# Copying x with its upper half already shifted by a token, one transpose per batch, and feed-forward weights loaded inside the layer

## The chip, the cores and the metric

The kernel runs on one core of one Trainium2 chip. A core has a matrix engine (PE in the profile; PEld is its weight load), a vector engine (DVE), a scalar engine (ACT), a GpSimd engine (POOL) and a sync engine (SP) that here only issues DMAs. Each runs its own instruction stream in order and waits on semaphores. The metric is device time in microseconds (us), lower is better.

## The reference, cut to what matters

The program is a small transformer: x is 16 batches of 128 tokens by 128 features. A first attention, a mixture of experts and a second cross-attention come first (about the first quarter of the time). Then come six layers, which the change is about:

```python
def shift_tokens(t):
    a, s = jnp.split(t, 2, -1)
    s = jnp.pad(s, ((0, 0), (1, 0), (0, 0)))[:, :-1]
    return jnp.concatenate([a, s], -1)
...
for i in range(DEPTH):                       # DEPTH = 6
    x = attn_layer(shift_tokens(x), Wqkv[i], q_scale[i], k_scale[i], Wo[i]) + x
    x = ffn_layer(shift_tokens(x), ln_g[i], ln_b[i], W1[i], b1[i], W2[i], b2[i]) + x
```

`attn_layer` projects to q, k and v (16 heads of 64), normalises q and k, applies rotary tables, attends in windows of 32 tokens to the own window and the one before, and projects back. `ffn_layer` is layer norm, a gated hidden layer of 341 features, and a projection back. `shift_tokens` leaves features 0 to 63 of a token and takes features 64 to 127 from the token before; token 0 gets zeros.

## The kernel before, in words

`Y` holds x in on-chip memory, tokens on the partitions. In each layer the attention goes through 64 units: a unit is one of the 16 batches and four of the 16 heads. On each engine a `Pipeline` lays out the stages of a unit, each stage some slots behind the first, so that one slot of PE holds a stage of each of several units. A layer is: 8 opening slots written out (`nxt.start(...)`, the first four of them woven into the feed-forward part of the layer before), a loop of 7 turns of 8 slots (`att.steady()`), and the closing slots woven into the feed-forward part of the same layer. That feed-forward part works on 4 groups of 4 batches. The layers 0 to 4 are the body of an outer loop (`Fori(0, LAYERS - 1)`) which begins with `att.steady()`; the last layer is written out behind it.

The PE order within a slot is: scores (mask L850, products L858), transposes of q and k (L831, 4), probabilities times values (`l_pv`, L878, 32 small products), projection of q and k (L814), of v (L823), output projection (L898), transposes of the result (L888, 2), transposes of the probabilities (L841, 2), and in every fourth slot `l_turn_x` (L802 and L803). `l_turn_x` reads `xin`, a copy of one batch of `Y`, and puts its transpose into the bank: the lower 64 features by a product with the identity, the upper 64 by a product with a shifted identity, which is the token shift. ACT and DVE split the turned x into two parts for the projections.

SP serves the layers by a written-out order (`serve_layer`). Per batch it issues twice four DMAs that move values to other partitions (`move_values`, L360: `stash<-l_v`), as soon as ACT has copied the v of two units (L1179), and one DMA `xin<-Y` (`take_x`, L365) for the batch after next. PE's `l_pv` of every second unit waits for the four moves. During the first three batches of a layer SP also loads the projection weights of the next layer (L330). After the last batch it waits for the output projections, loads `l_wo`, waits for the first feed-forward group, copies x of two batches of the next layer, then waits until all four feed-forward groups are done and issues the 12 DMAs of the next layer's feed-forward weights (`load_feed_forward`, L336 to L347). Only behind these come the first `move_values` of the next layer. The engines wait for these weights (`ld_fw`) at the start of the feed-forward part of the layer.

Of the kernel before, what the change touches and what calls it, by code (L numbers as in the profile page):

```python
# [20 lines left out]
B, S, D = 16, 128, 128  # L21
HALF = D // 2
# [68 lines left out]
def build(nc, t, out):  # L91
    with ExitStack() as ctx:
        def sb(name, shape, dt=F32):
            return ctx.enter_context(nc.sbuf_tensor(name, shape, dt))

        def sem(name):
            return ctx.enter_context(nc.semaphore(name))

        def upto(before, n):

            return before + (max(n, 0) if isinstance(n, int) else n) + CREDIT


        bank = ctx.enter_context(nc.psum_tensor("bank", [128, 8, 512], F32))
        X = sb("X", [128, B, D])
        Y = sb("Y", [128, B, D])
# [6 lines left out]
        ident = const[:, K_IDENT:K_IDENT + 128]  # L115
        shift_t = const[:, K_SHIFT:K_SHIFT + 128]
# [93 lines left out]
        xin = sb("xin", [128, 2, D])  # L210

        l_ss = sb("l_ss", [128, 2, 8, 2])
# [29 lines left out]
        preset = sem("preset")  # L242
        moved = [[sem(f"moved{k}{q}") for q in range(2)] for k in range(2)]
        ld_xin = [sem(f"ld_xin{k}") for k in range(2)]
# [8 lines left out]
        def stage_sems(prefix, names):  # L253

            made = {n: sem(prefix + n) for n in names.split()}
            stage_all.extend(made.values())
            return made
# [9 lines left out]
        l = stage_sems("l_", core.replace("sub_done ", "") + "w_high_done w_split "  # L267
                 "x_turned x_high_done x_split qk_proj v_proj rot_done sq_done ss_done floored logged guessed newton rn_done "
                 "add_done qk_done qk_turned qkT_done v_done o_turned oT_done out_done res_done")
        f = stage_sems("f_", "xs stats stat pool_st rstd n_done turned nT_done hidden gelu_done h_done out_mm yb_done "  # L270
                 "y_done")
# [3 lines left out]
        def apart(eng):  # L275


            eng.sem_inc(passed[eng.engine], 1)

        def one(t3, b):  # L280

            return t3[:, bass.ds(b, 1), :].rearrange("p a n -> p (a n)")
# [3 lines left out]
        def _(sp):  # L286
# [35 lines left out]
            def layer(name, ly):  # L322
                x = t["L1_ffn_" + name]
                v = x[bass.ds(ly, 1)]
                return v.rearrange("a b c -> (a b) c") if len(x.shape) == 3 else v.rearrange("a b -> (a b)")

            def load_projections(ly, *pieces):
                for piece in pieces:
                    at = slice(512 * piece, 512 * piece + 512)
                    sp.dma_start(l_raw[:, at], layer("Wqkv", ly)[:, at]).then_inc(ld_raw, 16)  # L330

            def load_output(ly):
                sp.dma_start(l_wo[:], layer("Wo", ly).rearrange("(c p) n -> p c n", p=128)).then_inc(ld_lw, 16)

            def load_feed_forward(ly):
                sp.dma_start(f_w1[:], layer("W1", ly)).then_inc(ld_fw, 16)  # L336
                full = FF // 128 * 128
                sp.dma_start(f_w2[:, 0:full // 128, :],
                             layer("W2", ly)[0:full].rearrange("(c p) n -> p c n", p=128)).then_inc(ld_fw, 16)
                sp.dma_start(f_w2[0:FF - full, full // 128, :], layer("W2", ly)[full:FF]).then_inc(ld_fw, 16)  # L340
                sp.dma_start(f_g[:, 0:1], layer("ln_g", ly).rearrange("(p a) -> p a", a=1)).then_inc(ld_fw, 16)
                sp.dma_start(f_g[:, 1:2], layer("ln_b", ly).rearrange("(p a) -> p a", a=1)).then_inc(ld_fw, 16)
                for s in range(2):
                    for k, (c0, n) in enumerate(CHUNKS):
                        sp.dma_start(f_b1[0:n, s, k:k + 1], layer("b1", ly)[s * FF + c0:s * FF + c0 + n]
                                     .rearrange("(p a) -> p a", a=1)).then_inc(ld_fw, 16)
                sp.dma_start(f_b2[:], layer("b2", ly).partition_broadcast(128)).then_inc(ld_fw, 16)  # L347

            def move_values(ly, b, k, q):

                ub, two = ly * UNITS, slice(2 * q, 2 * q + 2)
                sp.wait_ge(l["v_done"], upto(ub, 4 * b + 2 * q + 2))
                apart(sp)
                if not isinstance(b, int) or b >= 2:
                    sp.wait_ge(l["pv_done"], upto(ub, 4 * b + 2 * q - 6))
                    apart(sp)
                for dst, half, at in ((l_v2, 0, 32), (l_v2, 1, 32), (l_v3, 0, 64), (l_v3, 1, 0)):
                    sp.dma_start(dst[64 * half:64 * half + 64, k, two], l_v[at:at + 64, k, half, two])\  # L360
                      .then_inc(moved[k][q], 16)

            def take_x(ly, b, k):

                sp.dma_start(xin[:, k], one(Y, b)).then_inc(ld_xin[k], 16)  # L365

            def next_x(ly, b, k):
                sp.wait_ge(l["x_turned"], upto(ly * B, b + 1))
                apart(sp)
                take_x(ly, b + 2, k)  # L370

            def serve_layer(ly, last):

                for b in range(4):
                    for q in range(2):
                        move_values(ly, b, b % 2, q)
                        if q == 0:
                            next_x(ly, b, b % 2)
                        if not last and 2 * b + q < W_CHUNKS:
                            if b + q == 0:  # L380
                                sp.wait_ge(l["w_split"], upto(0, (ly + 1) * W_CHUNKS))
                                apart(sp)
                            load_projections(ly + 1, 2 * b + q)
                with sp.Fori(2, B // 2 - 1) as i:
                    for k in range(2):
                        move_values(ly, 2 * i + k, k, 0)
                        next_x(ly, 2 * i + k, k)
                        move_values(ly, 2 * i + k, k, 1)
                for b in range(B - 2, B):
                    for q in range(2):  # L390
                        move_values(ly, b, b % 2, q)
                if not last:
                    sp.wait_ge(l["out_done"], upto(0, (ly + 1) * B))
                    apart(sp)
                    load_output(ly + 1)
                    sp.wait_ge(f["y_done"], upto(0, ly * 4 + 1))
                    apart(sp)
                    for b in range(2):
                        take_x(ly + 1, b, b)
                    sp.wait_ge(f["y_done"], upto(0, (ly + 1) * 4))  # L400
                    apart(sp)
                    load_feed_forward(ly + 1)

            load_projections(0, *range(W_CHUNKS))
            load_output(0)
            load_feed_forward(0)
            sp.wait_ge(c["y_done"], upto(0, 2))
            for b in range(2):
                take_x(0, b, b)
            sp.wait_ge(c["y_done"], upto(0, B))  # L410
            with sp.Fori(0, LAYERS - 1) as ly:
                serve_layer(ly, False)
# [10 lines left out]
        def _(pool):  # L423
# [2 lines left out]
            pool.memset(c_v[:, :, :, :, C_DIM:], 1.0)  # L426
            pool.memset(l_v[:, :, :, :, :, L_DIM:], 1.0)
            pool.memset(m_p[:, :, EXPERTS:], -1.0)
            pool.memset(l_ss[:, :, :, 1:], 1e-24).then_inc(preset, 1)
            pool.wait_ge(preset, 1)  # L430

            def rstd(dst, var, chain, n, done):
# [158 lines left out]
        def _(pe):  # L591
# [180 lines left out]
            def attention(ly):  # L772
                ub, bb = ly * UNITS, ly * B

                def issued(mine, other, r):

                    at = [fn for _, fn in stages]
                    (s0, _), (s1, _) = stages[at.index(mine)], stages[at.index(other)]
                    return r + s0 - s1 + (at.index(other) < at.index(mine))
# [4 lines left out]
                def values_read(mine, b, r):  # L784

                    v, x = (issued(mine, fn, r) for fn in (l_project_v, l_turn_x))
                    pe.wait_ge(l["v_done"], upto(ub, no_more(4 * b + v, UNITS)))
                    pe.wait_ge(l["x_split"], upto(bb, no_more(b + (x + 3) // 4, B)))
# [5 lines left out]
                    pe.wait_ge(l["oT_done"], upto(ub, no_more(4 * b + turned, UNITS)))  # L794

                def l_turn_x(u, b, j):

                    if j % 4 == 0:
                        x = xin[:, j // 4]
                        pe.wait_ge(ld_xin[j // 4], (ly * B + b - j // 4) * 8 + 16)  # L800
                        values_read(l_turn_x, b, 0)
                        pe.matmul(bank[0:HALF, 1, 256:384], x[:, 0:HALF], ident, start=True, stop=True)  # L802
                        pe.matmul(bank[HALF:, 1, 256:384], x[:, HALF:], shift_t, start=True, stop=True)\  # L803
                          .then_inc(l["x_turned"], 1)

                high, low = (w[:].rearrange("p (t n) -> p t n", t=3) for w in (w_high, w_low))
                passes = ((0, high), (0, low), (1, high))
# [1001 lines left out]
```

## Time and profile before

| | us |
|---|---|
| median of 3 runs | 2393.64 |
| lowest, highest | 2389.98, 2394.75 |
| the profiled execution's own time | 2385.23 |
| span of the instructions in it | 2383.4 |
| mean granted clock of PE | 0.968 |

The profile shows one execution. Busy shares of the span are PE 93%, PEld 71%, DVE 72%, ACT 66%, POOL 59%. A granted clock of 1.00 is the upper of PE's two levels (2.4 GHz), 0.50 the lower (1.2 GHz). "idle <- X" is the time an engine stood idle until X released it; "issue" means that nothing that the profile shows was waited for.

### The profile page before, as it was taken

The page shows a single profiled execution, that of the slowest core. Times are in us where ns is not written, and L with a number is a line of the kernel's source. Part 1 is how long each engine was busy: PE and PEld are TensorE (multiplying, and loading weights), DVE is VectorE, ACT ScalarE, POOL GpSimd, SP SyncE. Part 2 cuts the span into 40 slices and gives each one's busy share as a digit, 9 for nine tenths or more (in the row PEclk, how much of TensorE's full clock was granted, in tenths as well). Part 3 has the DMA queues.
Part 4 walks back from the last instruction along what each step waited for, and adds up shares of the span by engine and source line. Part 5 has one row for each costly group of instructions (what it writes and reads, how often), then busy time and mean ns, then how long its engine had stood idle before and what let it go on. Part 6 is the DMA issues. An engine that isn't in the chain of part 4 may idle for free.

```text
span 2383.4 us, 105405 instructions
## 1 busy us (share of the span) xinstructions
PE 2211.0 (93%) x36645; PEld 1694.9 (71%) x36645; DVE 1725.2 (72%) x4617; ACT 1563.0 (66%) x5192; POOL 1412.3 (59%) x2638
## 2 busy tenths in 40 slices
PE   6998699998999979999799998999988999889998
PEld 4775277776888658886578875788756888578885
DVE  4777788886777657786577865677756788568884
ACT  3554455565888548886478873788746888468883
POOL 3443611115888538885378863688726888278882
PEclk9998899998999989999999999999998999999999
DMA  3000000011111112111111111211102111021110
GB/s 98 0 0 1 0 1 0 0 48 43 49 39 40 31 42 54 40 40 33 43 50 40 40 29 34 63 40 39 34 21 71 40 39 38 14 50 40 40 38 22
DMA packets 107749, 82.51 MB, mean 35 GB/s; under 512 B 26422, under 2 KB 100292, under 8 KB 107588
## 3 DMA queue, kind: packets, MB, share of 16 engines
q1 hardware_dynamic: 107588, 80.46, 12.9%
q8 instruction: 89, 1.46, 0.3%
q14 instruction: 72, 0.59, 0.1%
HBM read 21.94 MB, written 1.05 MB: 10 GB/s over the span
## 4 chain that ended last, share of the span: by engine, by line
PE 74%; DVE 4%; issue 4%; SPq 2%; ACT 1%; POOL 1%; DMA 0%; DVEq 0%; ACTq 0%; POOLq 0%
PE bank L814 14%; PE bank L831 9%; PE bank L898 7%; PE bank L878 6%; PE bank L858 6%; PE bank L823 6%; PE bank L888 4%; PE bank L841 3%; PE bank L850 2%; PE bank L749 2%; PE bank L955 2%; PE bank L944 2%; PE bank L945 2%; PE bank L738 2%; PE bank L597 1%
## 5 line engine op out<-in xcount | busy, mean ns | idle before, releaser
L530 POOL TENSOR_TENSOR l_qk<-l_rot 128x512 f32<-128x512 f32 x384 | 494.4, 1287 | 134.0 <-PE bank L831 60.6
L1202 ACT ACTIVATE l_qkT<-bank 128x512 f32<-128x512 f32 x384 | 229.8, 599 | 278.2 <-PE bank L831 278.2
L1580 DVE TENSOR_TENSOR l_rot<-bank,l_tab 128x512 f32<-128x512 f32 x384 | 265.0, 690 | 197.8 <-ACT l_sq L1186 197.8
L551 POOL TENSOR_TENSOR l_qk<-l_qk,l_rn 128x512 f32<-128x512 f32 x384 | 400.9, 1044 | 0.9
L1166 ACT ACTIVATE prob<-bank,peak 128x64 f32<-128x64 f32 x1536 | 355.0, 322 | 1.3 <-DVE peak L1602 1.3
L814 PE MATMUL bank<-w_high,xs_part 128*128 128x512 f32 x768 | 351.8, 458 | 3.2 <-DVE xs_part L1571 2.8
L1186 ACT ACTIVATE l_sq<-bank 128x512 f32<-128x512 f32 x384 | 237.1, 617 | 55.9 <-PE bank L814 44.8
L1584 DVE TENSOR_TENSOR l_rot<-bank,l_tab 128x512 f32<-128x512 f32 x384 | 261.5, 681 | 0.0
L831 PE MATMUL bank<-const,l_qk 128*128 128x128 f32 x1536 | 255.2, 289 | 5.3 <-POOL l_qk L551 5.2
L1594 DVE TENSOR_REDUCE l_ss<-l_sq 128x8 f32<-128x512 f32 x384 | 259.8, 677 | 0.2
L898 PE MATMUL bank<-l_wo,l_oT 128*128 128x128 f32 x1536 | 239.0, 279 | 0.0
L823 PE MATMUL bank<-w_high,xs_part 128*128 128x256 f32 x768 | 202.9, 286 | 11.6 <-issue 11.6
L878 PE MATMUL bank<-l_v,probT 64*32 64x65 f32 x4608 | 179.5, 225 | 35.2 <-DMA stash<-l_v 22.8
L898 PEld LDWEIGHTS bank<-l_wo,l_oT 128*128 128x128 f32 x1536 | 206.3, 193 | 3.3 <-issue 0.3
L1602 DVE TENSOR_REDUCE peak<-bank 128x4 f32<-128x256 f32 x384 | 160.8, 419 | 50.7 <-PE bank L858 43.4
L831 PEld LDWEIGHTS bank<-const,l_qk 128*128 128x128 f32 x1536 | 163.5, 142 | 41.4 <-POOL l_qk L551 6.8
L878 PEld LDWEIGHTS bank<-l_v,probT 64*32 64x32 f32 x4608 | 117.2, 108 | 105.3 <-issue 105.3
L814 PEld LDWEIGHTS bank<-w_high,xs_part 128*128 128x128 f32 x768 | 146.8, 191 | 62.2 <-issue 5.8
L435 POOL TENSOR_SCALAR ln_rs<-ln_mv 128x1 f32<-128x1 f32 (+1 forms) x64 | 14.5, 227 | 273.5 <-DVE ln_mv L1548 128.3
L858 PE MATMUL bank<-l_qkT 64*32 64x64 f32 x12288 | 175.8, 223 | 0.0
L878 PE MATMUL bank<-stash,probT 64*32 64x65 f32 x7680 | 174.5, 226 | 0.0
L1619 DVE TENSOR_TENSOR o<-bank,rsum 128x256 f32<-128x256 f32 x384 | 163.1, 425 | 13.3
(202 smaller groups left out, 5374.8 us busy)
## 6 DMA issues: line engine op xcount, KB each, us to landing
stash<-l_v SPq DMA_DIRECT2D x768, 65.0 KB, 2.0
early<-in_L_ffn_Wqkv_dram SPq DMA_DIRECT2D x36, 256.0 KB, 3.2
xin<-Y SPq DMA_DIRECT2D x96, 64.0 KB, 1.8
l_wo<-in_L_ffn_Wo_dram SPq DMA_DIRECT2D x6, 512.0 KB, 3.8
f_w<-in_L_ffn_W_dram SPq DMA_DIRECT2D x6, 341.0 KB
out_dram<-X SPq DMA_DIRECT2D x4, 256.0 KB, 2.3
f_w<-in_L_ffn_W_dram SPq DMA_DIRECT2D x6, 128.0 KB
l_oT<-in_L_xattn_Wkv_dram SPq DMA_DIRECT2D x1, 512.0 KB, 6.1
```

The costliest lines, as they stand in the source:

```text
L530: pool.tensor_tensor(l_qk[:, k], l_rot[:, k, 0], l_rot[:, k, 1], ALU.add).then_inc(l["add_done"], 1)
L551: pool.tensor_tensor(v, v, l_rn[:, k, :, None].broadcast_to([128, 8, L_DIM]), ALU.mult).then_inc(l["qk_done"], 1)
L814: ins = pe.matmul(bank[:, 0, :].rearrange("p (q n) -> p q n", q=2), xs_part[:, part, j // 4], w[:, 0:2, 256 * g:256 * g + 256], start=n == ...
L823: ins = pe.matmul(bank[:, 1, 0:256], xs_part[:, part, j // 4], w[:, 2, 256 * g:256 * g + 256], start=n == 0, stop=n == 2)
L831: ins = pe.transpose(bank[:, 2, n * 128:(n + 1) * 128], l_qk[:, j % 2, n * 128:(n + 1) * 128], ident)
L858: ins = pe.matmul(bank[w * WINDOW:(w + 1) * WINDOW, 3 + r, BAND * p:BAND * (p + 1)], l_qkT[rows, j % 2, queries:queries + WINDOW], l_qkT[r ...
L878: ins = pe.matmul(bank[w * WINDOW:(w + 1) * WINDOW, 6 - p, at:at + L_DIM + 1], probT[rows, j % 2, 128 * r + w * WINDOW:128 * r + (w + 1) * ...
L898: ins = pe.matmul(bank[:, 7, 256:384], l_oT[:, j // 4, p], l_wo[:, p], start=p == 0, stop=p == 7, skip_group_check=True)
L1166: ins = act.activation(prob[:, k, n * BAND:(n + 1) * BAND], bank[:, 3 + r, p * BAND:(p + 1) * BAND], ACT.Exp, bias=peak[:, k, n:n + 1])
L1580: dve.tensor_tensor(l_rot[:, k, 0].rearrange("p (q h n) -> p q h n", q=2, h=4), bank[:, 0, :].rearrange("p (q h n) -> p q h n", q=2, h=4), ...
L1584: dve.tensor_tensor(l_rot[:, k, 1].rearrange("p (q h s n) -> p q h s n", q=2, h=4, s=2), bank[:, 0, :].rearrange("p (q h s n) -> p q h s n ...
L1594: dve.tensor_reduce(l_ss[:, k, :, 0], l_sq[:].rearrange("p (h n) -> p h n", n=L_DIM), AX.X, ALU.add)\
```

## The change: what it does

1. `take_x` issues two DMAs in place of one: the lower 64 features of all 128 tokens, and the upper 64 features of tokens 0 to 126 into the rows of tokens 1 to 127. The row of token 0 is set to zero once, at the program's start, by POOL.
2. `l_turn_x` is then one transpose of `xin` in place of the two products. PE waits for two landings per batch, so its count is 32 for each batch, and 32 for the first, where it was 16.
3. The 12 DMAs of the feed-forward weights of a layer are issued inside that same layer, behind the moves of its fourth batch, and no longer at the end of the layer before (for the first layer: no longer ahead of the layers). The wait for all four feed-forward groups moves from the end of the layer to the third batch of the next one, ahead of the copy of x for its fifth batch.

```diff
             def take_x(ly, b, k):
-                sp.dma_start(xin[:, k], one(Y, b)).then_inc(ld_xin[k], 16)
+                x = one(Y, b)
+                sp.dma_start(xin[:, k, 0:HALF], x[:, 0:HALF]).then_inc(ld_xin[k], 16)
+                sp.dma_start(xin[1:, k, HALF:], x[0:S - 1, HALF:]).then_inc(ld_xin[k], 16)
...
             def serve_layer(ly, last):
                 for b in range(4):
+                    if b == 2:
+                        sp.wait_ge(f["y_done"], upto(0, ly * 4))
+                        apart(sp)
                     for q in range(2):
                         move_values(ly, b, b % 2, q)
...
                             load_projections(ly + 1, 2 * b + q)
+                load_feed_forward(ly)
                 with sp.Fori(2, B // 2 - 1) as i:
...
                     for b in range(2):
                         take_x(ly + 1, b, b)
-                    sp.wait_ge(f["y_done"], upto(0, (ly + 1) * 4))
-                    apart(sp)
-                    load_feed_forward(ly + 1)
 
             load_projections(0, *range(W_CHUNKS))
             load_output(0)
-            load_feed_forward(0)
...
-            pool.memset(l_ss[:, :, :, 1:], 1e-24).then_inc(preset, 1)
+            pool.memset(l_ss[:, :, :, 1:], 1e-24)
+            pool.memset(xin[0:1, :, HALF:], 0.0).then_inc(preset, 1)
...
                     if j % 4 == 0:
-                        x = xin[:, j // 4]
-                        pe.wait_ge(ld_xin[j // 4], (ly * B + b - j // 4) * 8 + 16)
+                        pe.wait_ge(ld_xin[j // 4], (ly * B + b - j // 4) * 16 + 32)
                         values_read(l_turn_x, b, 0)
-                        pe.matmul(bank[0:HALF, 1, 256:384], x[:, 0:HALF], ident, start=True, stop=True)
-                        pe.matmul(bank[HALF:, 1, 256:384], x[:, HALF:], shift_t, start=True, stop=True)\
-                          .then_inc(l["x_turned"], 1)
+                        pe.transpose(bank[:, 1, 256:384], xin[:, j // 4], ident).then_inc(l["x_turned"], 1)
```

The order of SP at the end of a layer's body before: the output weights (L333), x for two batches (L365), and then the feed-forward weights (L336 onward); L411 closes the outer loop, whose body begins with the moves L360.

```order
L333 DMA l_wo<-in_L_ffn_Wo_dram 128x8x128
L396 ISA
L365 DMA xin<-Y 128x128 x2
L400 ISA
L336 ISA
L336 DMA f_w<-in_L_ffn_W_dram 128x682
```

The same place now: the lines of x are L367 and L368, and the loop closes (L414) right behind them.

```order
L333 DMA l_wo<-in_L_ffn_Wo_dram 128x8x128
L403 REGISTER_ALU
L367 DMA xin<-Y 128x64
L368 DMA xin<-Y 127x64
L367 DMA xin<-Y 128x64
L368 DMA xin<-Y 127x64
L414 REGISTER_ALU
L414 COMPARE_AND_BRANCH
```

So the moves of the next layer's first batch follow the copies of x directly, and SP no longer passes the 12 weight DMAs between them.

SP before, from the fourth batch's second group of moves to the loop over the later batches (L384):

```order
L365 DMA xin<-Y 128x128
L354 REGISTER_ALU
L360 DMA stash<-l_v 64x260 x4
L384 UNCONDITIONAL_BRANCH
L384 ISA
```

And now:

```order
L368 DMA xin<-Y 127x64
L354 REGISTER_ALU
L360 DMA stash<-l_v 64x260 x4
L336 ISA
L336 DMA f_w<-in_L_ffn_W_dram 128x682
L338 ISA
L338 DMA f_w<-in_L_ffn_W_dram 128x2x128
L340 ISA
L340 DMA f_w<-in_L_ffn_W_dram 85x128
```

The twelve DMAs (nine more rows follow, up to L347) now stand between the moves of the fourth and of the fifth batch.

PE before, at the end of a slot that turns x and the start of the next:

```order
L841 MATMUL bank<-const,prob 128x128 x2
L800 ISA
L787 ISA
L802 MATMUL bank<-const,xin 64x128
L803 MATMUL bank<-const,xin 64x128
L850 MATMUL bank<-l_mask,cbf 128x128 x2
```

And now (the lines have moved by a few numbers, L804 is the transpose):

```order
L841 MATMUL bank<-const,prob 128x128 x2
L802 ISA
L791 ISA
L804 MATMUL bank<-const,xin 128x128
L850 MATMUL bank<-l_mask,cbf 128x128 x2
```

One instruction of the program stands where two stood, with the same neighbours; nothing else moves on PE.

## Rows read from the trace of the kernel before

**Rows 1.** Busy time by engine, an opening and a stretch in the loop.

```profile
core 0: us, PE busy (x) PEld busy (x) DVE busy (x) ACT busy (x) POOL busy (x), PEclk, DMA share, GB/s
861.00:870.00 9.00, 6.77 (x106) 5.03 (x104) 6.15 (x13) 5.13 (x18) 7.93 (x18) 1.00 0.27 61
1000.00:1100.00 100.00, 99.47 (x2257) 80.85 (x2256) 79.83 (x200) 82.01 (x302) 82.35 (x160) 1.00 0.15 39
```

**Rows 2.** PE in order of time, slots in the loop: start, us, what.

```profile
914.41 0.38 PE L841 MATMUL bank<-const,prob 128*128 128x128 f32 x2
914.62 0.28 PE L850 MATMUL bank<-l_mask,cbf 128*128 128x128 bf16 x2
...
922.06 0.38 PE L841 MATMUL bank<-const,prob 128*128 128x128 f32 x2
922.37 0.32 PE L802 MATMUL bank<-const,xin 128*64 128x128 f32 x1
...
922.74 0.28 PE L850 MATMUL bank<-l_mask,cbf 128*128 128x128 bf16 x2
```

**Rows 3.** Landing of the DMAs of xin, all 96.

```profile
DMA to landing us min/median/max: 1.8/1.8/4.6
```

**Rows 4.** Waits of the whole span: us in total, times, longest.

```profile
PE bank L878 <- DMA stash<-l_v: 22.8, 5, 4.9
...
PEld bank L802 <- ACT l_v L1179: 19.3, 86, 1.3
...
PE bank L850 <- issue: 15.8, 4, 4.8
```

**Rows 5.** ACT and SP in order of time, end of the first layer.

```profile
858.07 0.37 ACT L1179 ACTIVATE l_v<-bank 128x256 f32<-128x256 f32 x1
...
862.77 0.35 SPq L336 DMA_DIRECT2D f_w<-in_L_ffn_W_dram  x1
...
870.28 2.43 SPq L360 DMA_DIRECT2D stash<-l_v  x4
```

**Rows 6.** PE in order of time, same place.

```profile
867.88 0.28 PE L850 MATMUL bank<-l_mask,cbf 128*128 128x128 bf16 x2
...
874.32 0.28 PE L878 MATMUL bank<-l_v,probT 64*32 64x65 f32 x1 [4.90 <-DMA stash<-l_v]
...
886.81 0.28 PE L850 MATMUL bank<-l_mask,cbf 128*128 128x128 bf16 x2 [4.10 <-issue]
```

**Rows 7.** The same two slots in each of the six layers.

```profile
573.66:580.73 7.07, 6.96 (x166) 5.58 (x164) 5.91 (x15) 5.75 (x23) 6.09 (x13) 1.00 0.20 56
867.88:886.81 18.93, 9.71 (x167) 7.46 (x164) 7.17 (x16) 6.40 (x23) 6.89 (x13) 0.73 0.37 98
1173.58:1190.64 17.06, 9.13 (x166) 7.13 (x164) 7.18 (x16) 6.29 (x23) 6.90 (x13) 0.80 0.42 108
1481.57:1499.56 17.99, 9.01 (x166) 7.00 (x164) 7.17 (x16) 6.29 (x23) 6.76 (x13) 0.78 0.40 104
1789.02:1806.12 17.10, 8.71 (x166) 6.86 (x164) 7.17 (x16) 6.29 (x23) 6.76 (x13) 0.79 0.42 109
2096.30:2109.49 13.19, 8.56 (x167) 6.93 (x164) 6.27 (x15) 6.50 (x25) 6.74 (x13) 0.74 0.31 75
```

**Rows 8.** The next slot, layers two to five, summed; and layer six.

```profile
sum 26.80, PE 25.54 PEld 19.55 DVE 11.43 ACT 16.45 POOL 14.70; mean PE 6.38 PEld 4.89 DVE 2.86 ACT 4.11 POOL 3.67
...
2109.49:2113.58 4.09, 4.09 (x90) 3.16 (x88) 3.34 (x9) 3.52 (x14) 3.31 (x8) 1.00 0.05 14
```

**Rows 9.** SP, ACT, PE in order of time, later in layer two.

```profile
902.45 0.51 SPq L365 DMA_DIRECT2D xin<-Y  x1
...
929.50 0.40 ACT L1179 ACTIVATE l_v<-bank 128x256 f32<-128x256 f32 x1
...
930.19 2.41 SPq L360 DMA_DIRECT2D stash<-l_v  x4
...
942.39 0.24 PE L878 MATMUL bank<-l_v,probT 64*32 64x65 f32 x1
```

## The prediction

> **What bounds the kernel now.** I read the busy time by engine first. In the loop over the units PE is busy 99.47 of 100 us at the upper clock, and POOL, the next, 82.35 [rows 1]. So inside the loop any time taken off PE's stream comes off the total, and time on the others does not. Then the waits of PE: two kinds are large and sit between layers. PE's first product with moved values (L878) waits 22.8 us in five places for a DMA, `stash<-l_v`, and PE stands 15.8 us in four places ahead of L850 for "issue", that is for nothing the profile shows [rows 4]. Third, SP and ACT in order of time say why the DMA is late: ACT has copied the v of the layer's first two units by 858.44, but SP issues their moves only at 870.28, because from 862.77 on it issues the 12 feed-forward weight DMAs, and before that it waited for the last feed-forward group [rows 5]. PE goes on at 874.32 after 4.90 us of standing [rows 6]. Fourth, the windows of the same two slots in each layer (from L850 of the second unit to L850 of the fourth) show what the stop costs in full: 7.07 us in the first layer, which has no such stop, but 18.93, 17.06, 17.99, 17.10 and 13.19 in the others, with a mean granted clock of 0.73 to 0.80 and not 1.00 [rows 7]. A clock below 1 here means that part of the stretch ran at the lower level, 1.2 GHz, behind the stop.
>
> **The transpose.** There are 96 turns of x, 16 a layer. Today, from the first of the two products to the next instruction of PE (L850) it is 922.74 - 922.37 = 0.37 us. Two transposes of the same size, L841 up to L850, take 914.62 - 914.41 = 0.21, so 0.105 each [rows 2]. The saving is 0.37 - 0.105 = 0.265 us a turn. Of the 16 turns of a layer 15 stand in attention slots, where PE is the bound: 90 x 0.265 = 23.9 us. The other six stand in the feed-forward part or ahead of the first layer, where PE also waits; they give 0 to 1.6 us, and I take 0. The wait ahead of the turn for ACT's copy of v, 19.3 us in 86 places at the weight load, has nothing to do with how x is turned and stays [rows 4]. The trace has no lone transpose between an ordinary one and the bf16 products. From below: two transposes show 0.38 us of which the first takes 0.11 of issue, so one lasts 0.27 to its end; if nothing of that overlapped, the turn would save 0.10 us, 9 us in all. From above: it cannot cost less than nothing, 0.37 x 96 = 35.5. I take 23.9, because the row of two transposes in the same place is by far the nearest.
>
> A rule speaks against this. The Trainium skill, page "TensorE: Matmul & The Clock Gate", section "PE-mode transpose", gives about 275 ns for a 128x128 transpose in a kernel's context. By it a turn would save 0.37 - 0.275 = 0.095 us (an estimate from that page), 8.6 us in all. The rows contradict it as a rate: two follow each other in 0.21. Its figure is close to the 0.27 that one lasts from start to end.
>
> **The copy of x in two pieces.** Each batch has one more DMA on SP's queue, 0.51 us (the first copy's own issue is that long [rows 9]). x of a batch is issued at 902.45 and turned at 922.37 [rows 2, 9], 19.9 us later, and lands after 1.8 us, at worst 4.6 [rows 3]. Even twice that leaves 10 us. The extra issue stands behind the first four moves of its batch and ahead of the second four, which are not due yet: per batch of four slots, some 15 us, the queue is busy 2 x 2.41 + 2 x 0.51 = 5.8 us [rows 9]. Cost taken: 0; without this cover it would be 0.51 x 96 = 49 us. It can't gain, since nothing waits for x now. The zeroing of one row on POOL at the start is one small instruction: 0.
>
> **The layer boundary.** With the 12 DMAs gone from there, the first moves can be issued when v is there, 858.44, not 870.28: 11.8 us earlier, so they land at about 862.5, and PE needs them at 869.4 (874.32 - 4.90) [rows 5, 6]. The wait goes wholly, in all five boundaries. What is late next: in the opening POOL is busy 7.93 of 9.00 us [rows 1], so it nearly sets the pace, with about the same slot length as PE. For the two slots I take the first layer's 7.07 us, plus the stop of 15.8 us in four places, which belongs to the jump back to the start of the outer loop: it shows in layers two to five and not in the first and the sixth, which are entered without that jump [rows 4, 7]. Before: 18.93 + 17.06 + 17.99 + 17.10 + 13.19 = 84.27. After: 5 x 7.07 + 15.8 = 51.2. The difference is 33.1; I take off 2 us for POOL, which will be up to one unit further behind than today, when it catches up during PE's stop: 31 us. Of these 22.8 are the wait itself and the rest is work that runs at the upper clock. From below: POOL's lateness takes back half of it, 15 us; from above 33.1 and what follows.
>
> The slot behind the jump takes 26.80 us in the four layers and 4.09 in layer six, so 26.80 - 4 x 4.09 = 10.4 us more, at the lower clock [rows 8]. The stop before it stays, so I count this at 0 gain. If the fuller stretch ahead of the stop keeps the clock up, up to 10.4 us come on top. On the stop itself: the Trainium skill, page "Runtime: NRT & Kernel Launch", section "Instruction fetch mechanics", says that a taken branch whose target is not in the fetched window stalls until the code is fetched. By it the 15.8 us stay whatever came before the branch; if instead the stop were a late effect of the DMA wait, the sum would be 15.8 + 10.4 larger. Rows 7 side with the rule: layer six has the DMA wait and no such stop.
>
> **The weights inside the layer.** The 12 issues now stand between the moves of the fourth and the fifth batch. Today's fifth batch: v is copied at 929.90, the moves are issued 930.19 to 932.60, land 1.6 us later (at the boundary the last of four is issued at 872.71 and PE goes on at 874.32), and PE needs them at 942.39: 8.2 us to spare [rows 6, 9]. The 12 DMAs hold SP from 862.77 to 870.28, 7.5 us [rows 5]. They start 2.7 us (0.3 and 2.4) after the v copy of the moves before, which is two slots, 7.07 us or a little more, ahead of this one; so they end 2.7 + 7.5 - 7.07 = 3.1 us after the fifth batch's v copy, in place of 0.3. Of 8.2 us some 5.4 remain. Cost: 0, with the 12 DMAs allowed to take 13 us before PE waits. The weights are wanted only at the layer's end. At the end of the body SP has less to do, and that is in the boundary's sum.
>
> **The sum.** 23.9 + 31 = 55 us. Against the profiled execution, 2385.2 us (span 2383.4 and 1.8 around it), that gives 2330; this execution lies 8.4 below the median of the runs, so against 2393.6 it gives 2338.6, 2339 rounded. About 0.2% (4.8 us) is what a measurement of this kernel tells from no change.
>
> **Rivals.**
> - *The transpose costs its whole length* (0.27 us and not 0.105): the turns give 9 us, 15 less: 2354. For it: it stands alone between two other kinds of product. Against: L841 to L850 shows no such price. 0.09.
> - *The opening is bound by POOL, ACT and DVE once PE no longer stops*: the boundary gives 15 to 23 us in place of 31: 2347 to 2355. For it: POOL's 7.93 of 9.00. Against: the first layer's 7.07 for the same slots. 0.12.
> - *The clock stays up behind the jump too*: 10.4 us more: 2328, with part of the stop 2320. For it: PE will be fuller before the stop. Against: the stop is as long as before. 0.11.
> - *Slower: the weight DMAs stall the fifth batch.* Their 12 issues, or their bytes ahead of the moves on the same DMA engines, hold the moves beyond the 13 us. It decides from there. In layer six a wait of 4.6 us costs 13.19 - 7.07 = 6.1 us, 1.33 times itself. To end above 2398 it takes 60 us, 10 a layer, a wait of 7.5, so a hold of 20 us; at 22 us it is 9 x 1.33 x 6 = 72 us: 2411. Against: the same 12 DMAs ahead of the same moves take 7.5 us at the boundary, and the moves land 1.6 us behind them. 0.02.
>
> **Numbers.** The forecast has 0.66, with its own range of 2331 to 2346. The range 2326 to 2354 takes in the clock rival's larger part and the two smaller gains. Faster by over 0.2%: 0.97; within: 0.01; slower: 0.02.
>
> **What would show it.** Right: no wait of L878 for `stash<-l_v`; the two slots at 7 to 8 us in layer six and at 10.5 to 12 in layers two to five; L841 to L850 in a turning slot shorter by 0.26; slots of the loop that do not turn x unchanged; "issue" ahead of L850 still four times about 4 us. Wrong: a wait for moved values in a layer's fifth batch; PE below 98% in the loop; POOL as what L831 waits for in the openings.

## The result and the profile after

The changed kernel takes 2330.86 us (median of 4 runs, 2329.66 to 2337.46), the kernel before beside it 2391.81 (4 runs). The ratio is 0.9753, 95% interval 0.9727 to 0.9778: faster by 2.5%. The forecast was 2339, with its own range of 2331 to 2346, whose lower edge the measured time just misses (by 0.1 us), and a wider range of 2326 to 2354, in which it lies.

| | before | after |
|---|---|---|
| median of the runs | 2391.81 | 2330.86 |
| the profiled execution's own time | 2385.23 | 2337.46 |
| span in it | 2383.4 | 2335.6 |
| mean granted clock of PE | 0.968 | 0.970 |

The profiled execution of after is the slowest of its four, and that of before lay below its median. So the two profiles differ by 47.8 us where the medians differ by 60.9. The 13 us between come back below, under "The total".

PE's waits after, over the whole span (us in total, times, longest), against [rows 4]:

```profile
PE bank L850 <- issue: 13.2, 4, 3.6
PE bank L823 <- issue: 11.6, 10, 1.9
PE bank L878 <- ACT probT L1174: 10.3, 8, 2.7
```

No wait of L878 for `stash<-l_v` is left: 22.8 us in five places have gone. The stop ahead of L850 (PE stands and the profile names nothing that it waits for) is still there four times, 13.2 us for 15.8.

The same two slots of each layer after, from L850 of the second unit to that of the fourth, first the first layer and then layers two to six. The columns are those of [rows 7]: the stretch, its length, busy time by engine, PE's granted clock, DMA share, GB/s.

```profile
578.49:586.04 7.55, 7.55 (x166) 5.96 (x164) 6.11 (x15) 5.70 (x22) 6.02 (x13) 0.90 0.15 45
869.02:879.47 10.45, 7.23 (x166) 5.51 (x164) 6.89 (x16) 5.94 (x23) 6.77 (x13) 1.00 0.34 97
1167.08:1177.60 10.52, 7.22 (x166) 5.50 (x164) 6.89 (x16) 5.94 (x23) 6.76 (x13) 0.99 0.35 94
1463.46:1474.41 10.95, 7.24 (x167) 5.51 (x164) 6.89 (x16) 5.93 (x23) 6.76 (x13) 0.99 0.32 90
1760.16:1770.83 10.67, 7.25 (x166) 5.51 (x164) 6.89 (x16) 5.93 (x23) 6.77 (x13) 1.00 0.33 92
2057.10:2064.27 7.17, 7.06 (x167) 5.56 (x165) 5.98 (x15) 6.13 (x25) 6.40 (x13) 1.00 0.23 59
```

In layers two to six they take 49.76 us where they took 84.27. PE's busy time fell too (7.2 for 9.7 in the second layer), because the same work now runs at the upper clock: 1.00 for 0.73. What is left above 7.2 us in four layers is the stop.

The slot behind the jump, layers two to five summed, against [rows 8]:

```profile
1474.41:1481.24 6.83, 6.53 (x85) 5.32 (x86) 2.99 (x7) 3.89 (x14) 3.65 (x9) 0.51 0.01 4
...
sum 29.35, PE 24.80 PEld 20.23 DVE 11.69 ACT 15.07 POOL 14.23; mean PE 6.20 PEld 5.06 DVE 2.92 ACT 3.77 POOL 3.56
```

It was 26.80, so nothing came back here; the granted clock in it is 0.51 to 0.59, close to the lower level. Stop and slot together are the same as before: 13.2 + 29.35 = 42.6, and 15.8 + 26.80 = 42.6. PE in order of time in a turning slot, against [rows 2]; L804 is the transpose:

```profile
901.96 0.38 PE L841 MATMUL bank<-const,prob 128*128 128x128 f32 x2
902.20 0.33 PE L804 MATMUL bank<-const,xin 128*128 128x128 f32 x1
902.36 0.28 PE L850 MATMUL bank<-l_mask,cbf 128*128 128x128 bf16 x2
```

From L841 to L850 it is 0.40 us; before it was 0.68 (922.06 to 922.74). The forecast had 0.265 less; it is 0.28 less. The slots of the loop that do not turn x take 3.60 us at the median, 3.61 before.

SP, ACT and PE around the weight DMAs in the second layer, against [rows 9]:

```profile
917.36 2.42 SPq L360 DMA_DIRECT2D stash<-l_v  x4
919.99 0.42 SPq L336 DMA_DIRECT2D f_w<-in_L_ffn_W_dram  x1
...
924.17 0.40 ACT L1179 ACTIVATE l_v<-bank 128x256 f32<-128x256 f32 x1
...
925.59 0.34 SPq L347 DMA_DIRECT2D f_b<-in_L_ffn_b_dram  x1
926.50 2.42 SPq L360 DMA_DIRECT2D stash<-l_v  x4
...
936.77 0.24 PE L878 MATMUL bank<-l_v,probT 64*32 64x65 f32 x1
```

The 12 DMAs hold SP for 6.5 us. The fifth batch's moves go out 1.9 us behind the copy of v (924.57) and their last issue ends at 928.92, 7.8 us before PE wants them. They land about 1.6 us after that issue, so 6.2 us are to spare; 5.4 were forecast.

### The profile page after: what moved, and what is told of

It reads as the page before. It is cut to its first block, busy times and chain, and to the rows that moved or that the text cites. A ratio compares the mean times of both kernels' runs of the same rounds, so it can differ in the third digit from the quotient of the medians.

```text
span 2335.6 us, 104987 instructions
## 1 busy us (share of the span) xinstructions
PE 2182.5 (93%) x36357; PEld 1691.0 (72%) x36357; DVE 1706.1 (73%) x4617; ACT 1557.1 (67%) x5192; POOL 1415.4 (61%) x2639
## 4 chain that ended last, share of the span: by engine, by line
PE 76%; DVE 4%; issue 4%; POOL 1%; ACT 1%; DVEq 0%; ACTq 0%; POOLq 0%
PE bank L814 14%; PE bank L831 9%; PE bank L898 7%; PE bank L878 6%; PE bank L858 6%; PE bank L823 6%; PE bank L888 4%; PE bank L841 4%; PE bank L753 2%; PE bank L955 2%; PE bank L945 2%; PE bank L850 2%; PE bank L944 2%; PE bank L742 2%; PE bank L601 2%
## 5 line engine op out<-in xcount | busy, mean ns | idle before, releaser
L831 PE MATMUL bank<-const,l_qk 128*128 128x128 f32 x1536 | 254.7, 289 | 4.5 <-POOL l_qk L555 4.3
L831 PEld LDWEIGHTS bank<-const,l_qk 128*128 128x128 f32 x1536 | 163.6, 142 | 40.4 <-POOL l_qk L555 6.1
L878 PE MATMUL bank<-l_v,probT 64*32 64x65 f32 x4608 | 177.7, 224 | 15.8 <-ACT probT L1174 10.3
L878 PEld LDWEIGHTS bank<-l_v,probT 64*32 64x32 f32 x4608 | 115.9, 107 | 85.6 <-issue 85.6
L1619 DVE TENSOR_TENSOR o<-bank,rsum 128x256 f32<-128x256 f32 x384 | 163.0, 425 | 13.2
L878 PE MATMUL bank<-stash,probT 64*32 64x65 f32 x7680 | 172.7, 224 | 0.0
```

What stands on the lines that cost most here:

```text
L831: ins = pe.transpose(bank[:, 2, n * 128:(n + 1) * 128], l_qk[:, j % 2, n * 128:(n + 1) * 128], ident)
L878: ins = pe.matmul(bank[w * WINDOW:(w + 1) * WINDOW, 6 - p, at:at + L_DIM + 1], probT[rows, j % 2, 128 * r + w * WINDOW:128 * r + (w + 1) * ...
```

## The experiments

Each ratio is to runs of the kernel before on the same chip.

**The two parts apart.** First the turn alone; the weights stay at the boundary.

```diff
-                    if b == 2:
-                        sp.wait_ge(f["y_done"], upto(0, ly * 4))
-                        apart(sp)
...
-                load_feed_forward(ly)
                 with sp.Fori(2, B // 2 - 1) as i:
...
+                    sp.wait_ge(f["y_done"], upto(0, (ly + 1) * 4))
+                    apart(sp)
+                    load_feed_forward(ly + 1)
...
+            load_feed_forward(0)
```

> The split copy of x and the one transpose, with the feed-forward weights still loaded at the layer boundary. Theory A (the two parts of the change do not touch each other): the turning slot of PE is 3.78 us in place of 4.07, 96 x 0.287 = 27 us less than before, and the wait of L878 for stash stays at 5 x 4.6 us. Ratio to before about 0.9885. Rival B (a turn saves only the 0.208 us between the first product and L850; the shorter gap ahead of it in the changed kernel came from elsewhere): 20 us, ratio 0.9917.

Measured: 2365.9 us, ratio 0.9906 (0.9884 to 0.9928). The turning slot is 3.78 us for 4.07, and PE's wait stays whole:

```profile
PE bank L878 <- DMA stash<-l_v: 22.7, 5, 4.9
PE bank L850 <- issue: 13.7, 4, 3.5
```

The slot says A (0.287 a turn). The time, with an interval wider than the difference between A and B, holds both. Only 84 of the 96 turns stand in such slots (14 a layer), so A's 27 us should have been 84 x 0.287 = 24.

Then the weights alone, with the copy and the two products of before:

```diff
-                x = one(Y, b)
-                sp.dma_start(xin[:, k, 0:HALF], x[:, 0:HALF]).then_inc(ld_xin[k], 16)
-                sp.dma_start(xin[1:, k, HALF:], x[0:S - 1, HALF:]).then_inc(ld_xin[k], 16)
+                sp.dma_start(xin[:, k], one(Y, b)).then_inc(ld_xin[k], 16)
...
-                        pe.transpose(bank[:, 1, 256:384], xin[:, j // 4], ident).then_inc(l["x_turned"], 1)
+                        pe.matmul(bank[0:HALF, 1, 256:384], x[:, 0:HALF], ident, start=True, stop=True)
+                        pe.matmul(bank[HALF:, 1, 256:384], x[:, HALF:], shift_t, start=True, stop=True)\
+                          .then_inc(l["x_turned"], 1)
```

> The feed-forward weights inside the layer, with the whole copy of x and the two products of before. Theory A: the five boundaries give 34.5 us (84.3 to 49.8 for the two slots), so 61 - 27 = 34 us less than before, ratio about 0.986, and no wait of L878 for stash. Rival B (only the wait itself goes, 22.8 us; the slower clock stays): ratio 0.9905.

Measured: 2354.5 us, ratio 0.9866 (0.9840 to 0.9892): A's 34 us; B's 0.9905 lies outside. No wait for stash is left. The two ratios multiply to 0.9773, against 0.9753 for both together, so the parts add up within the noise.

**The split copy against the transpose.** The shifted copy in two DMAs, turned by two half-width products:

```diff
-                        pe.transpose(bank[:, 1, 256:384], xin[:, j // 4], ident).then_inc(l["x_turned"], 1)
+                        x = xin[:, j // 4]
+                        pe.matmul(bank[0:HALF, 1, 256:384], x[:, 0:HALF], ident, start=True, stop=True)
+                        pe.matmul(bank[HALF:, 1, 256:384], x[:, HALF:], ident, start=True, stop=True)\
+                          .then_inc(l["x_turned"], 1)
```

> The changed kernel, but the already shifted copy is turned by two half-width products with the identity, the shape of before. It separates the two DMAs per batch from the transpose. Theory A (all of the turn's gain is PE's): the turning slot is 4.07 us again and the time is that of the weights-only kernel within 3 us, about 27 us above the changed kernel. Rival B (the split copy itself costs or gives time): it differs from the weights-only kernel by over 5 us.

Measured: 2356.0 us, ratio 0.9866 (0.9843 to 0.9889), the same as with the weights alone (2354.5), and the turning slot is 4.06 us. The extra DMA per batch costs nothing that can be measured; the turn's whole gain is PE's.

**Why the gap ahead of the turn closed.** One ordinary full-width product in place of the transpose:

```diff
-                        pe.transpose(bank[:, 1, 256:384], xin[:, j // 4], ident).then_inc(l["x_turned"], 1)
+                        pe.matmul(bank[:, 1, 256:384], xin[:, j // 4], ident, start=True, stop=True).then_inc(l["x_turned"], 1)
```

> The changed kernel, but one ordinary full-width fp32 product with the identity in place of the transpose (two passes on PE). Theory A (0.08 us ahead of the two half-width products was the price of going from full width to half width, not a wait for the copy of v): L841 to the turn is 0.11 to 0.13 us as with the transpose, the turn itself 0.22 to 0.27, the turning slot 3.85 to 3.90 us, some 8 us above the changed kernel. Rival B (the gap was a wait for v, or is tied to a two-pass product): the gap is 0.20 again and the slot 3.95 to 4.0, 18 us above the changed kernel.

Measured: 2343.6 us, ratio 0.9813 (0.9792 to 0.9834). PE in order of time there:

```profile
900.49 0.38 PE L841 MATMUL bank<-const,prob 128*128 128x128 f32 x2
900.73 0.49 PE L804 MATMUL bank<-const,xin 128*128 128x128 f32 x2
901.05 0.28 PE L850 MATMUL bank<-l_mask,cbf 128*128 128x128 bf16 x2
```

L841 (two) to the turn is 0.24 us, as with the transpose; with two half-width products it is 0.31 (922.06 to 922.37 in [rows 2]). Over all slots the gap behind the second L841 is 0.117 here, 0.122 with the transpose and 0.203 before. So the 0.08 us went with the half width, as A says, and did not depend on transpose or product. The program's waits ahead of the turn are the same in this kernel and in the one with the shifted copy and two products, whose gap is 0.202. Why two half-width products want 0.08 us more ahead of them is not shown. The turn itself came out dearer than A had it, 0.325 and not 0.22 to 0.27, and the slot 3.94, not 3.85 to 3.90. The time lies between A and B: by the ratios it is about 14 us above the changed kernel (0.9813 for 0.9753), and 84 slots of 0.16 us more are 13.

**Why a lone transpose takes 0.164 us.** It is issued twice into the same place:

```diff
-                        pe.transpose(bank[:, 1, 256:384], xin[:, j // 4], ident).then_inc(l["x_turned"], 1)
+                        for _ in range(2): ins = pe.transpose(bank[:, 1, 256:384], xin[:, j // 4], ident)
+                        ins.then_inc(l["x_turned"], 1)
```

> The changed kernel with the transpose of x issued twice into the same place. In the changed kernel a lone transpose holds PE for 0.164 us up to L850, where I had forecast 0.105 (0.21 for the two of L841). Theory A (the other 0.06 us is not the array's: PE's sequencer is behind, because it handles two waits ahead of the turn and more ahead of L850): the second transpose hides in it, turn to L850 is 0.22 and the turning slot 3.83 to 3.84 us in place of 3.78, 5 us above the changed kernel in all. Rival B (the change of operand kind ahead of L850 costs 0.06 us of PE's time): 0.27 and a slot of 3.89, 10 us above.

```profile
897.98 0.38 PE L842 MATMUL bank<-const,prob 128*128 128x128 f32 x2
898.22 0.44 PE L804 MATMUL bank<-const,xin 128*128 128x128 f32 x2
898.50 0.28 PE L851 MATMUL bank<-l_mask,cbf 128*128 128x128 bf16 x2
```

PE in order of time: from the turn to the next instruction it is 0.273 us at the median over 84 turns, so the second transpose adds 0.109, its full rate, and a fixed 0.055 stays. That is B's number, against my A. The turning slot is 3.89. What the 0.055 is stays open: B named the change of operand kind ahead of L850, but two transposes of `prob` go over to the same L850 at 0.109 each. What differs is the copy they read and the waits ahead of them. The time hardly followed the slots: 2333.17 us, ratio 0.9778 (0.9752 to 0.9805), where the changed kernel had 2333.19 and 0.9765 on another chip, an interval too wide to tell nothing from 10 us. In the profiles the layers are longer about as expected (10 us over the six, from the first unit to the last, against the second profile of the changed kernel), but all five feed-forward stretches between layers are shorter, 56 us in place of 57.8. The one behind the second layer, first in that profile and then here:

```profile
1102.84:1160.71 57.87, 49.03 (x316) 31.95 (x314) 31.03 (x78) 24.03 (x49) 14.69 (x22) 0.94 0.08 22
```

```profile
1103.43:1159.45 56.02, 47.72 (x318) 31.25 (x316) 31.14 (x79) 24.25 (x49) 14.20 (x22) 0.97 0.07 18
```

The granted clock is 0.94 and 0.97: one fall to the lower level less. In each of the five it is so. Such shifts of the clock can hide a change of 10 us here.

**Order on SP or bytes on the DMA engines.** The weights at the boundary again, but behind the first four moves:

```diff
-                    if b == 2:
-                        sp.wait_ge(f["y_done"], upto(0, ly * 4))
-                        apart(sp)
...
+                        if b + q == 0:
+                            sp.wait_ge(f["y_done"], upto(0, ly * 4))
+                            apart(sp)
+                            load_feed_forward(ly)
                         if q == 0:
                             next_x(ly, b, b % 2)
...
-                load_feed_forward(ly)
```

> The changed kernel, with the 12 weight DMAs issued at the boundary again, but behind the first four moves of the layer's first batch and not ahead of them; the wait for the last feed-forward group stands ahead of them too. Theory A (before, it was SP's order that delayed the first moves, not the bytes of the weights on the DMA engines): the first moves go out with v, PE does not wait for them; the second four moves are issued about 870 in the second layer and are needed after the stop at the jump, so no wait either: within 5 us of the changed kernel. Rival B (the weights' bytes at the boundary are what costs): a wait of L878 for stash of 3 us or more in each of five boundaries, 20 to 30 us above the changed kernel.

Measured: 2331.1 us, ratio 0.9760 (0.9743 to 0.9776); the changed kernel run beside it took 2333.2, ratio 0.9765. No wait for stash. SP in order of time at the same boundary, against [rows 5]:

```profile
854.23 2.44 SPq L360 DMA_DIRECT2D stash<-l_v  x4
860.10 0.36 SPq L336 DMA_DIRECT2D f_w<-in_L_ffn_W_dram  x1
...
865.97 0.33 SPq L347 DMA_DIRECT2D f_b<-in_L_ffn_b_dram  x1
```

The same bytes move at the same place; only the first four moves now stand ahead of the twelve loads, and ahead of the wait for the last feed-forward group too. It was the order. Of the 11.8 us by which the moves were late before, 7.5 are the twelve loads and 4.3 the wait ahead of them (858.44 to 862.77 in [rows 5]); the two were not taken apart.

**How much cover there is.** 24 small DMAs more behind the weights:

```diff
                 load_feed_forward(ly)
+                for n in range(24):
+                    sp.dma_start(spare[:, n:n + 1], layer("b1", ly)[0:128].rearrange("(p a) -> p a", a=1)).then_inc(ld_fw, 16)
...
-        FW_DMAS = 5 + 2 * len(CHUNKS) + 1
+        FW_DMAS = 24 + 5 + 2 * len(CHUNKS) + 1
```

> The changed kernel with 24 further small DMAs (0.5 KB each, into a tile nothing reads) behind the 12 weight DMAs of each layer, so SP is held 6.5 + 24 x 0.49 = 18.3 us between the moves of the fourth and the fifth batch. In the changed kernel the fifth batch's moves end 7.8 us before PE needs them and land 1.6 us after issue: 6.2 us to spare. Theory A (the cover is time on SP's queue): 11.8 - 6.2 = 5.6 us of wait in each of six layers, with the slower clock 1.33 times that, 45 us above the changed kernel, about 2376. Rival B (the queue is not what holds the moves, or later waits swallow it): less than 10 us above.

Measured: 2380.6 us, ratio 0.9967 (0.9950 to 0.9983), 47 us above the changed kernel beside it (45 expected). The wait over the span, and SP in order of time; L361 and L881 are the moves and PE's reader here:

```profile
PE bank L881 <- DMA stash<-l_v: 37.2, 6, 7.2
```

```profile
930.53 11.39 SPq L393 DMA_DIRECT2D spare<-in_L_ffn_b_dram  x24
942.48 2.43 SPq L361 DMA_DIRECT2D stash<-l_v  x4
```

Six waits of 6.2 us; 5.6 were expected. This is the slower rival made real, as far as it is time on the queue. The hold is 18.0 us, so by subtraction the wait begins at about 12 us of hold, where the forecast put 13; at 18 it gives back nearly all of the change. In the profiles the six layers are 52 us longer than in the changed kernel's second profile, 1.4 times the 37.2 us of waiting, and the feed-forward stretches between them 7 us shorter, so the match of 47 with 45 is in part chance.

**The stop at the jump.** The outer loop over the layers written out on all five engines, the inner loops kept:

```diff
-            with pe.Fori(0, LAYERS - 1) as ly:
+            for ly in range(LAYERS - 1):
```

> The changed kernel with the outer loop over the first five layers written out on all five engines (the inner loops stay). Theory A (the stop ahead of L850 belongs to the jump back to the outer loop's start): the stops (13.2 us) go, the slot behind them is 3.8 us in place of 7.3 on average (14.2 us), and the slots of the inner loops, which in the last layer save 0.31 us a loop turn, do so in all (10.8 us): 38 us below the changed kernel, about 2293. Rival B (the stop is the engines' catching up at the boundary, or longer straight code stops PE elsewhere for fetching): less than 10 us below, or slower.

Measured: 2288.3 us (2287.15 to 2290.3), ratio 0.9579 (0.9563 to 0.9595); 45 us below the changed kernel beside it. This is the fastest version, 1.9% below the changed kernel. The two slots in the second and the sixth layer:

```profile
861.63:868.82 7.19, 7.02 (x166) 5.58 (x164) 5.91 (x15) 6.17 (x25) 6.43 (x13) 1.00 0.30 83
2007.77:2015.05 7.28, 6.99 (x166) 5.57 (x164) 5.91 (x15) 6.13 (x25) 6.57 (x13) 1.00 0.15 38
```

The stop is gone in every layer, the slot behind it takes 3.8 us, and from the 13th to the 57th unit it is 160.7 to 160.8 us in every layer, where it is 162.3 to 162.5 in the changed kernel's first five. That is A, with 7 us more than it had. Against the second profile of the changed kernel the six layers are 37 us shorter, A's 38, and 6 us come from the feed-forward stretches between them, where the clock fell less often. The code being longer cost nothing that can be seen.

The same with the kernel before (the five loops written out in it):

> The kernel before (whole copy, two products, weights loaded at the boundary) with the outer loop over the layers written out. It tells whether the stop at the jump and the wait for the moves are separate. Theory A (they are): the stops (15.8 us), the slower slot behind them (10.4) and the dearer slots of the inner loops (35 loop turns x 0.3 = 10.5) go, the five waits of L878 for stash of 4.6 us stay: 37 us below the kernel before, ratio 0.9846. Rival B (without the jump the engines reach the boundary otherwise and the wait shrinks or the stop was partly the wait's): 45 us or more below, ratio under 0.981, or a wait for stash of under 15 us in all.

Measured: 2341.1 us, ratio 0.9811 (0.9784 to 0.9839), 47 us below the kernel before.

```profile
PE bank L878 <- DMA stash<-l_v: 17.2, 5, 3.9
```

The five waits stay but are shorter, 3.4 us for 4.6. The time lies outside A's ratio and at the edge of B's (0.9811 for under 0.981); B's other sign, a wait under 15 us, did not come. The shorter wait goes with SP: from the first weight DMA to the first move it is 5.1 to 6.2 us at the five boundaries, 5.6 on average, and before 6.5 to 7.5, on average 7.0. That fixed addresses in place of those worked out from the loop's counter make the issues shorter is likely, but was not tried apart. So the wait and the stop are separate costs: one stays without the outer loop, the other does not, and the loop made the wait longer. Without the outer loop the change gains 55 us by the ratios (0.9811 to 0.9579), with it 56 to 59 (0.9765 and 0.9753); the intervals do not tell these apart.

**A second profile of the changed kernel.**

> The changed kernel once more, as the yardstick for the three others on this chip and for a second profile: its first profile showed the lower clock for 30.7 us around the start of the layers. Theory A (that stretch was this execution's): 2331 us, and the second profile opens the layers 3 to 7 us earlier. Rival B (it belongs to the kernel): the same stretch again, and a profiled time of 2337.

Measured: 2333.19 us (2331.86 to 2335.42), ratio 0.9765 (0.9748 to 0.9781). L850 of the first layer's second unit stands at 576.07 in it, at 578.49 in the first profile and at 573.66 before. One window, 545 to 600 us, in before, after and this run:

```profile
545.00:600.00 55.00, 46.09 (x705) 36.57 (x705) 34.91 (x82) 30.82 (x110) 32.66 (x63) 0.81 0.20 54
```

```profile
545.00:600.00 55.00, 45.24 (x615) 36.28 (x615) 33.18 (x79) 27.51 (x96) 29.26 (x57) 0.72 0.17 45
```

```profile
545.00:600.00 55.00, 44.82 (x686) 35.91 (x686) 34.20 (x82) 29.43 (x102) 30.62 (x62) 0.78 0.18 49
```

The granted clock is 0.81, 0.72 and 0.78. Part of the first profile's slow opening was that execution's, as A says, though it was 2.4 us and not 3 to 7. Where the other 2.4 us against the kernel before come from is open.

## Why the prediction was right

**The boundary** (31 us taken, 33.1 worked out). In the profiles it is 84.27 - 49.76 = 34.5 us, and the kernel with the weights alone is 34 us faster. Of the 34.5 the stop's 2.6 are lost again in the slot behind it, which leaves 31.9. The first layer's 7.07 us was the right stand-in: layer six took 7.17. The 2 us taken off for POOL were not needed: L831 waited for POOL only once, 4.3 us ahead of the first layer, and does so before the change too. That more than the 22.8 us of waiting would go was the step that mattered: some 9 us more are the same work at the upper clock (PE's busy time in these slots).

**The turn** (23.9 us taken). The sum came out right by luck: three errors cancel. First, the turn's own saving was over-sized: a lone transpose holds PE 0.164 us, not 0.105, so 0.208 is saved and not 0.265. Second, the step "the wait ahead of the turn for ACT's copy of v has nothing to do with how x is turned and stays" was wrong. The view put 19.3 us of PEld's idle time in 86 places down to the copy of v; after the change it is this:

```profile
PEld bank L804 <- ACT l_v L1179: 6.3, 5, 1.3
```

With one full-width instruction the gap on PE fell from 0.203 to 0.122 us. Both together make 0.287 a turn. Third, not 90 turns stand where PE is the bound but 84: ahead of the turn in each layer's opening PE waits 0.5 to 1.1 us for ACT. 84 x 0.287 is 24 us. In the profiles the six layers are 55.6 us shorter, and without the boundary's 31.9 that leaves 23.6 for the turns. The kernel with the turn alone was 22 us faster, its interval 17 to 28. The transpose lasts 0.33 us in the row and holds PE for 0.16. The Trainium skill, "TensorE: Matmul & The Clock Gate", section "PE-mode transpose", gives about 275 ns for one; the trace does not agree with that as a price.

**The split copy** (0). Right: 2356.0 against 2354.5.

**The weights inside the layer** (0, with 13 us of allowance). Right, and the allowance nearly: 6.2 us to spare were found where 5.4 were forecast, and a hold of 18 us gave waits of 6.2, so the wait begins at about 12 us and not 13.

**The stop and the slot behind it** (0 gain). Right in kind. The stop fell from 15.8 to 13.2, the slot rose from 26.80 to 29.35, at a granted clock of 0.51 to 0.59: the rival that the clock stays up is out. In the kernels with the outer loop written out the stop is gone, so it belongs to the outer loop and, by its place, to the jump. The Trainium skill, "Runtime: NRT & Kernel Launch", section "Instruction fetch mechanics", puts such a stall down to the fetching of code behind a taken branch; these runs agree with it as far as the branch goes and do not show the fetching.

**The total.** 31.9 + 23.6 = 55.5 us in the layers, for 54.9 forecast. The two profiles differ by 47.8 only, because 7.8 us are lost outside the layers: the first layer opens 4.6 us later after the change, the five feed-forward stretches between layers sum to 289.0 for 287.4 us, and what follows the last unit's L850 takes 51.6 for 49.9. In all three the clock falls, at another moment and not equally often in each execution: the shortest of the five stretches before, 56.0 us, has one fall, and all the others, from 57.3 us on, have two. The medians differ by 60.9, 5 us more than the layers explain; the changed kernel measured again was 55.8 us below the kernel before (2333.19 for 2389.03). So the predicted 2339 was 8 us above the measured time for reasons outside the sum: the kernel before was 1.8 us faster beside this run (2391.81 for 2393.64), 0.6 are the layers, and the other 5 to 6 are of the size of such shifts.

## What to carry to other kernels

When a DMA is late, look first at what stands ahead of it in its queue: four moves put ahead of twelve weight loads, and of the wait before these, were worth the same as moving the loads away. Price a wait on the matrix engine by the window around it in an execution without it, since the slower clock behind it added two fifths here (31.9 us lost for 22.8 of waiting). And look once at what is left: a stop at an outer loop's jump, 13 us in four places, stood beside the wait in the same view, and writing that loop out gave another 45 us with the slower slots that went with it.

## What the runs showed of the hardware

- Two half-width fp32 products (64 columns of weights each, side by side) hold PE for 0.37 us and cost 0.08 us more ahead of them than a full-width instruction does. One full-width fp32 product takes 0.325, one transpose 0.164, a second transpose 0.109 more.
- 24 DMAs of 0.5 KB take 11.39 us of SP's queue, 0.47 each; twelve weight DMAs of 0.58 MB in all take 6.5, 0.54 each. The size hardly counts for the queue.
- In the inner loops a turn costs PE some 0.3 us more inside the outer loop than when the layer is written out (162.3 to 162.5 for 160.7 us over 5.5 turns).
- Writing out the outer loop took 45 to 47 us off both kernels, and the longer code showed no cost.
